# A transformer block with attention and feed forward: the output projection starts between the last values, and the feed forward's first half chunks stand under the last tile's normalisation

## What is computed

```python
mod = silu(c) @ wmod                        # sa, ca, ga, sb, cb, gb; |ga|, |gb| at least 0.25
h = layernorm(x) * (1 + ca) + sa
q, k, v = latent projections of h           # q from 128, k and v from 32 latent channels, rotary part of 64
attn = softmax(causal(q @ k.T * scale)) @ v # 32 heads
x = x + ga * (attn @ wo.T)                  # output projection
h = layernorm(x) * (1 + cb) + sb
gate = silu((h @ gate_w.T) * gate_s)        # 1376 hidden channels, int32 weights of -127..127
up = (h @ up_w.T) * up_s
x = x + gb * ((gate * up) @ down_w.T) * down_s
```

## Time and profile before

| | |
|---|---|
| time, median of 3 runs | 812.67 us (810.3 to 815.13) |
| profiled execution, its own time | 812.95 us |
| its span, first to last instruction | 810.8 us |
| granted TensorE clock over the span | 0.987 |
| TensorE busy | 759.1 us, 94% |
| VectorE busy | 553.5 us, 68% |
| ScalarE busy | 275.2 us, 34% |
| GpSimd busy | 152.5 us, 19% |

### The profile page before, as it was taken

The page is one execution under the profiler, slowest core; times in us unless marked ns, Lnnn a source line. Parts: engine busy times, 40 slices in busy tenths (PEclk is TensorE's granted clock), DMA queues, the critical chain, the costliest instruction groups (busy, mean ns, idle before and its releaser), DMA issues.

```text
span 810.8 us, 10303 instructions
## 1 busy us (share of the span) xinstructions
PE 759.1 (94%) x3901; PEld 497.4 (61%) x3901; DVE 553.5 (68%) x831; ACT 275.2 (34%) x394; POOL 152.5 (19%) x132
## 2 busy tenths in 40 slices
PE   3898899999999999999999999997997999999997
PEld 1755465555555555555555556453886788886886
DVE  6877679789789789789789779599464222223342
ACT  3722233433433433433433333444243222222210
POOL 1136413023023023023023000101242000000111
PEclk9999899999999999999999999999998999999999
DMA  8333613303303303303303380252000132210011
GB/s 307 155 78 78 149 23 78 86 9 79 85 9 79 86 9 78 80 15 79 84 10 79 71 342 3 105 209 78 1 1 0 50 107 78 78 30 0 27 40 39
DMA packets 36144, 60.72 MB, mean 75 GB/s; under 512 B 4256, under 2 KB 16288, under 8 KB 34304
## 3 DMA queue, kind: packets, MB, share of 16 engines
q1 hardware_dynamic: 36096, 60.06, 26.5%
HBM read 32.66 MB, written 2.10 MB: 43 GB/s over the span
## 4 chain that ended last, share of the span: by engine, by line
PE 53%; DVE 31%; issue 11%; POOL 3%; ACT 2%; DMA 1%; POOLq 0%; SPq 0%; DVEq 0%; ACTq 0%
PE PS L769 15%; DVE PR L1269 8%; DVE NMa L1172 7%; PE PS L739 6%; PE PS L612 5%; PE PS L675 5%; PE PS L690 4%; PE PS L676 4%; PE PS L677 4%; DVE NMb L1172 3%; DVE wide L1269 3%; PE PS L628 2%; PE PS L602 1%; PE PS L679 1%; PE PS L616 1%
## 5 line engine op out<-in xcount | busy, mean ns | idle before, releaser
L905 ACT ACTIVATE PR<-PS 128x1024 f32<-128x1024 f32 (+1 forms) x144 | 133.0, 929 | 258.1 <-PE PS L677 232.2
L1172 DVE TENSOR_REDUCE NMa<-PS 128x1 f32<-128x512 f32 (+3 forms) x216 | 137.8, 660 | 34.4 <-PE PS L616 31.0
L612 PE MATMUL PS<-KH,Q 96*128 96x512 f32 (+3 forms) x384 | 130.6, 400 | 3.5 <-DVE TQ L1157 1.5
L675 PE MATMUL PS<-Q,KH 97*128 97x512 f32 x288 | 130.7, 454 | 0.0
L769 PE MATMUL PS<-Q 128*128 128x512 f32 (+1 forms) x528 | 123.2, 395 | 5.1 <-DVE Q L1368 4.5
L769 PEld LDWEIGHTS PS<-Q 128*128 128x128 f32 (+1 forms) x528 | 99.3, 188 | 28.2 <-DVE Q L1368 4.7
L1269 DVE TENSOR_TENSOR PR<-PR 128x2048 f32<-128x2048 f32 (+3 forms) x56 | 110.4, 1971 | 6.9 <-ACT PR L905 5.5
L676 PE MATMUL PS<-Q,KL 96*128 96x512 f32 x288 | 114.3, 397 | 0.0
L677 PE MATMUL PS<-Q,KH 96*128 96x512 f32 x288 | 113.7, 395 | 0.0
L612 PEld LDWEIGHTS PS<-KH,Q 96*128 96x128 f32 x384 | 67.7, 191 | 56.0 <-issue 29.2
L675 PEld LDWEIGHTS PS<-Q,KH 97*128 97x128 f32 x288 | 55.9, 194 | 25.6 <-issue 13.7
(11 more groups left out here) (177 smaller groups left out, 944.4 us busy)
## 6 DMA issues: line engine op xcount, KB each, us to landing
Q<-TQ SPq DMA_DIRECT2D x64, 384.0 KB, 5.6
RT<-in_wo SPq DMA_DIRECT2D x4, 1024.0 KB, 4.9
TQ<-in_wo SPq DMA_DIRECT2D x4, 1024.0 KB, 4.8
WI<-in_gate_w SPq DMA_DIRECT2D x10, 256.0 KB, 3.3
WI<-in_up_w SPq DMA_DIRECT2D x10, 256.0 KB, 3.7
DI<-in_down_w SPq DMA_DIRECT2D x10, 256.0 KB, 3.8
PR<-in_wmod_c SPq DMA_DIRECT2D x2, 1024.0 KB, 6.5
x_in<-in_x SPq DMA_DIRECT2D x8, 256.0 KB, 9.7
```

The lines of the kernel that those rows point to most:

```text
L612: ins = pe.matmul(bank[:, i * w:(i + 1) * w], M.Q[0:KR, g % 2, 0, qt // 4, h0 + i, qs], M.KH[0:KR, lo:lo + w], start=(i == 0), stop=(i == ...
L675: pe.matmul(dst, M.KH[0:KR + 1, ks], M.Q[0:KR + 1, w % 2, 0, qb, :, qs], start=True, stop=False)
L905: act.activation(tiles, banks, ACT.Exp).then_inc(S_.p, 1)
L1172: dve.tensor_reduce(dst, PS[:, bank_of(turn), 0:n * w].rearrange("p (h k) -> p h k", k=w), axis=AX.X, op=ALU.max, negate=True).then_inc(S_ ...
```

## The change

- In the last window the planner's table gets `high` of tiles 0 and 1 at places 0.84 and 0.90, with cost 0: ScalarE makes the high part there, GpSimd (no longer VectorE) the low part. AH and AL move to other memory for this (`rotated`, over buffers of the rotary part, the folding and the floor).
- `products` is cut into thirds (`product_term`, 8 matmuls each) in banks of the side rotation. TensorE's order is: first third of product 0, values of step 10, second third, values of step 11, last third, denominators, then product 1 and on as before. `turn_hidden` uses banks 1 and 3.
- Chunk 0 of the feed forward is split between tiles 4 and 5 of the projection (its split weights lie where the keys were). Behind the turning of tile 6, TensorE makes the first half of the positions of chunk 0 (24 matmuls), the turning of tile 7, the first half of chunk 1, then both second halves. The split of chunk 1 stands ahead of tile 7's normalisation.
- Gate and up loads, and down loads, have semaphores of their own; SP waits for each apart.
- `down` uses banks 4 and 5; before it TensorE waits for chunk 9 only, and for the last chunk's down weights within tile 0.
- The last tile is scaled, added and stored in two halves of 256 columns; the second half is added on VectorE.

```diff
@@ -255,9 +258,11 @@
-        self.at = big
+        self.at = rotated
         self.AH = take("AH", [P, 2, G, P], F32R)
         self.AL = take("AL", [P, 2, G, P], F32R)
+        assert self.at <= folded_end
+        self.at = big
@@ -344,6 +351,7 @@
     if w == G - 1:
+        places += group_places(w, [(0.84 + 0.06 * st, ("high", st), 0.0) for st in range(2)])
@@ -508,18 +524,26 @@
-    load_chunk(0)
-    load_chunk(1)
+    for ch in range(2):
+        load_gates(ch)
+        load_down(ch)
     for ch in range(2, NCH):
         sp.wait_ge(S_.fl, ch - 1)
+        load_gates(ch)
         sp.wait_ge(S_.fdl, ch - 1)
-        load_chunk(ch)
...
+    sp.wait_ge(S_.ot, NS)
+    sp.dma_start(out[last, 0:D // 2], M.OT[:, 1, 0:D // 2]).then_inc(S_.st[1], 16)
+    sp.wait_ge(S_.oh, 1)
+    sp.dma_start(out[last, D // 2:D], M.OT[:, 1, D // 2:D]).then_inc(S_.st[1], 16)
@@ -724,20 +748,20 @@
-    for s in LATE_VALUES:
-        values(G - 1, s)
-    denominator(G - 1, 1)
...
+    def product_term(st, n):
+        b = st % 2
+        if n == 0:
+            pe.wait_ge(S_.al, st + 1)
+            if st >= 2:
+                pe.wait_ge(S_.yr, st - 1)
+        a, w = ((M.AH, M.MH), (M.AL, M.MH), (M.AH, M.ML))[n]
+        for g in range(G):
+            ins = pe.matmul(PS[:, out_bank(st), :], a[:, b, g, :], w[:, g, :], start=(n == 0 and g == 0),
+                            stop=(n == 2 and g == G - 1))
+        if n == 2:
+            ins.then_inc(S_.y, 1)
...
     for b in range(3):
-        pe.wait_ge(S_.free[b], (len(TURN) + 2 - b) // 3)
-    for st in range(NS):
-        products(st)
-        if st > 0:
-            turn_hidden(st - 1)
+        pe.wait_ge(S_.free[b], (len(TURN) + 1 - b) // 3)
+    for n, s in enumerate(LATE_VALUES):
+        product_term(0, n)
+        values(G - 1, s)
+    for n in range(len(LATE_VALUES), 3):
+        product_term(0, n)
+    denominator(G - 1, 1)
+    pe.wait_ge(S_.p, NEXP * G)
+    for st in range(1, NS):
+        for n in range(3):
+            product_term(st, n)
+        turn_hidden(st - 1)
...
             pe.wait_ge(S_.hl, 2 * st + 1 + rest)
+            if rest and st == 0:
+                pe.wait_ge(S_.fdl, NCH)
...
+    pe.wait_ge(S_.fl, 1)
+    pe.wait_ge(S_.lo2, NS // 2)
+    gate_up(0, 0)
+    turn_hidden(NS - 1)
+    pe.wait_ge(S_.fl, 2)
...
+    gate_up(1, 0)
+    pe.wait_ge(S_.lo2, NS)
+    gate_up(0, 1)
+    gate_up(1, 1)
...
+    pe.wait_ge(S_.fhid, NC)
+    pe.wait_ge(S_.fdl, NC)
@@ -961,31 +1014,32 @@
-    attn_high(0)
-    for st in range(NS):
-        if st < NS - 1:
+    for st in range(NS - 1):
+        if 2 <= st + 1:
             attn_high(st + 1)
         if st > 0:
             modulate2(st - 1)
-        if st < NS - 1:
-            root2(st)
+        root2(st)
+        if st == NS // 2:
+            chunk_high(0)
...
     act.wait_ge(S_.y, NS)
-    chunk_high(0)
+    chunk_high(1)
+    modulate2(NS - 2)
     root2(NS - 1)
-    chunk_high(1)
     modulate2(NS - 1)
@@ -1349,24 +1403,30 @@
     sums_copied(G - 1, 1)
     invert(G - 1, 1)
-    attn_low(0)
-    for st in range(NS):
-        if st < NS - 1:
+    dve.wait_ge(S_.al, 2)
+    for st in range(NS - 1):
+        if 2 <= st + 1:
             attn_low(st + 1)
         gated(st)
         if st > 0:
             h2_high(st - 1)
-        if st < NS - 1:
-            normalise2(st)
...
+        normalise2(st)
+        if st == NS // 2:
+            chunk_low(0)
+    gated(NS - 1)
+    chunk_low(1)
+    h2_high(NS - 2)
+    normalise2(NS - 1)
+    h2_high(NS - 1)
@@ -1420,6 +1477,9 @@
         gated2(st)
+    dve.wait_ge(S_.yr2, NS + 1)
+    dve.wait_ge(S_.st[1], 16 * (NS // 2 - 1))
+    dve.tensor_tensor(M.OT[:, 1, D // 2:D], M.x1[:, NS - 1, D // 2:D], M.Y2[:, 1, D // 2:D], ALU.add).then_inc(S_.oh, 1)
@@ -1513,6 +1573,14 @@
+    def attn_low_first(st):
+        pool.wait_ge(S_.gt, 8)
+        pool.wait_ge(S_.ah, st + 1)
+        pool.tensor_tensor(M.AL[:, st % 2], M.attn[:, :, st * P:(st + 1) * P], M.AH[:, st % 2].bitcast(F32),
+                           ALU.subtract).then_inc(S_.al, 1)
```

More of the change, by code:

```diff
@@ L726, in pe_program @@
                 side(name)
-    for s in LATE_VALUES:
-        values(G - 1, s)
-    denominator(G - 1, 1)
-    def products(st):
+    def product_term(st, n):
         b = st % 2
[L734 to L740, removed]
+        if n == 0:
[8 more added lines that the diff above has]
+            ins.then_inc(S_.y, 1)
     def turn_hidden(st):
@@ L747, in turn_hidden, with gate_up, gate_or_up @@
         for d in range(KD):
[L748 removed]
+            ins = pe.transpose(PS[:, 1 + 2 * b, d * P:(d + 1) * P], M.xn2[:, b, d * P:(d + 1) * P], M.ident[:])
         ins.then_inc(S_.tr2, 1)
     for b in range(3):
[L752 to L775 removed]
+        pe.wait_ge(S_.free[b], (len(TURN) + 1 - b) // 3)
[10 more added lines that the diff above has]
+        turn_hidden(st - 1)
+    def gate_up(ch, hf):
+        b, m = ch % 2, P if ch < NC else IT
+        for w in range(2):
+            gate_or_up(ch, hf, w, b, m)
+    def gate_or_up(ch, hf, w, b, m):
+        for n, (a, h) in enumerate(((M.FH, M.h2H), (M.FL, M.h2H), (M.FH, M.h2L))):
+            for k in range(KD):
+                ins = pe.matmul(PS[0:m, 4 * b + 2 * w + hf, :], a[b][:, w, k, 0:m],
+                                h[:, k, hf * 512:(hf + 1) * 512],
+                                start=(n == 0 and k == 0), stop=(n == 2 and k == KD - 1))
+        if hf == 1:
+            ins.then_inc((S_.fg, S_.fu)[w], 1)
     def down(st):
@@ L785, in down @@
                 for ch in chunks:
-                    ins = pe.matmul(PS[:, b, :], a[b][0:k, ch, :], w[0:k, ch, :],
+                    ins = pe.matmul(PS[:, 4 + b, :], a[b][0:k, ch, :], w[0:k, ch, :],
                                     start=(n == 0 and ch == 0), stop=(n == 2 and rest == 1))
         ins.then_inc(S_.y2, 1)
-    for ch in range(NCH):
-        gate_up(ch)
-    pe.wait_ge(S_.fhid, NCH)
-    pe.wait_ge(S_.fdl, NCH)
+    pe.wait_ge(S_.fl, 1)
[3 more added lines that the diff above has]
+    pe.wait_ge(S_.fl, 2)
+    pe.wait_ge(S_.yr, NS)
+    pe.wait_ge(S_.o, 2 * G)
+    for b in range(3):
+        pe.wait_ge(S_.free[b], (len(TURN) + 2 - b) // 3)
+    gate_up(1, 0)
+    pe.wait_ge(S_.lo2, NS)
+    gate_up(0, 1)
+    gate_up(1, 1)
+    for ch in range(2, NCH):
+        pe.wait_ge(S_.fl, ch + 1)
+        pe.wait_ge(S_.fhid, ch - 1)
+        b, m = ch % 2, P if ch < NC else IT
+        for w in range(2):
+            for hf in range(2):
+                gate_or_up(ch, hf, w, b, m)
+    pe.wait_ge(S_.fhid, NC)
+    pe.wait_ge(S_.fdl, NC)
     for st in range(NS):
@@ L886, in side, with attn_high @@
             split_high(key[1], key[2])
+        elif key[0] == "high":
+            attn_high(key[2])
+    def attn_high(st):
+        act.wait_ge(S_.no, 2 * (G - 1) + st * P // QB + 1)
+        if st == 0:
+            act.wait_ge(S_.side, TURN[("fold", G - 1, G - 1)] + 1)
+        if st >= 2:
+            act.wait_ge(S_.y, st - 1)
+        act.activation(M.AH[:, st % 2], M.attn[:, :, st * P:(st + 1) * P], ACT.Copy).then_inc(S_.ah, 1)
     def exponentials(w, e):
@@ L1350, in h2_high, with chunk_low @@
         dve.tensor_copy(M.h2H[:, :, st * P:(st + 1) * P], M.full2[:, st % 2]).then_inc(S_.hi2, 1)
+    def chunk_low(ch):
+        b, m = ch % 2, P if ch < NC else IT
+        dve.wait_ge(S_.fh, ch + 1)
+        dve.tensor_tensor(M.FL[b][:, :, :, 0:m], M.WI[:, b, :, :, 0:m], M.FH[b][:, :, :, 0:m].bitcast(F32),
+                          ALU.subtract).then_inc(S_.fl, 1)
     sums_copied(G - 1, 1)
     invert(G - 1, 1)
-    attn_low(0)
-    for st in range(NS):
-        if st < NS - 1:
+    dve.wait_ge(S_.al, 2)
+    for st in range(NS - 1):
+        if 2 <= st + 1:
             attn_low(st + 1)
@@ L1400, in gated2 @@
             dve.wait_ge(S_.ot, st - 1)
-        dve.scalar_tensor_tensor(out=M.Y2[:, b], in0=PS[:, b, :], scalar=M.ffn_s[:, 2:3], in1=M.gate_b[:],
-                                 op0=ALU.mult, op1=ALU.mult).then_inc(S_.yr2, 1)
-    chunk_low(0)
-    normalise2(NS - 1)
-    chunk_low(1)
-    h2_high(NS - 1)
+        for cols in (slice(0, D),) if st < NS - 1 else (slice(0, D // 2), slice(D // 2, D)):
+            dve.scalar_tensor_tensor(out=M.Y2[:, b, cols], in0=PS[:, 4 + b, cols], scalar=M.ffn_s[:, 2:3],
+                                     in1=M.gate_b[:, cols], op0=ALU.mult, op1=ALU.mult).then_inc(S_.yr2, 1)
     hidden(0)
@@ L1515, in side @@
             normalise(g, key[2])
+        elif kind == "high":
+            attn_low_first(key[2])
+    def attn_low_first(st):
[3 more added lines that the diff above has]
+                           ALU.subtract).then_inc(S_.al, 1)
     for st in range(NS + 1):
```

62 lines of the change are left out of this document (29 added, 33 removed).

## The result

The changed kernel takes **802.13 us** (median of 4 runs, 801.23 to 803.38), the kernel before beside it 813.65 (4 runs, 810.3 to 815.13): a ratio of 0.9866, 95% interval 0.9844 to 0.9888. It is faster. The forecast was 802.4. The execution that was profiled took 803.38 us around a span of 801.6, against 812.95 around 810.8: 9.2 us less of span, where the working of the prediction had 10.5.

A forecast was written before the change was run, and what follows sets the result against it. From 566.5 us the chain was taken as TensorE nearly throughout, with waits and slow-clock stretches to remove. Gains 1.5 - 0.7 + 7.8 + 1.4 + 0.5 = 10.5 took 812.95 to 802.4 us; range 797.5 to 805.8.

The forecast's parts named there:

- the feed forward's start: From product 7's end to the last gate matmul: 121.1 us instead of 128.94, 7.8 gained.
- down: Before the down matmuls: the first 30 no longer wait for the last chunk, 1.4 us gained.
- the last store: At the kernel's end: storing the last tile in halves puts the last issue 0.5 us earlier, 0.5 gained.
- The exclusion in the last window: End of attention: GpSimd's low parts and VectorE's two-SBUF-input work exclude each other, making the last additions 3.6 us late.
- Rival 2: End of attention: GpSimd's low parts cost VectorE nothing, product 2 starts 2.3 us earlier, 797.9 us; chance 0.10.
- the one from product 1 to product 2: Projection's start: gating to normalisation takes 4.2 us, and product 2 starts at 576.8 instead of 580.29.
- Chunk 0's split: Mid-projection, after tile 4's root: the earlier split delays the low part of tile 6, 0.7 us lost once.
- The clock: Around products 0 and 1: one fall to half clock in the new gaps, at the old price, 2.3 us lost.
- rival 1: Gaps around products 0 and 1: no fall of the clock, 2.3 us better, 800.2 us; chance 0.33.
- rival 3: Gaps around products 0 and 1: two clock falls, 3.2 and 2.3 us, giving 805.7 us; chance 0.12.
- Rival 4: End of attention: a late GpSimd low part blocks the values behind product 0's first third, 804.4 to 806.4 us; chance 0.04.
- Rival 5: Projection: the clock falls at 561 and is not regained, matmuls take twice as long, up to 841 us; chance 0.02.

The follow-up runs named there:

- run 7: Changed kernel with TensorE's old order behind product 7 (tile 7 turned after 12 matmuls, whole chunks), chunk 0's early split kept: 806.93 us.
- run 6: Changed kernel with the old end: TensorE waits for the last chunk before down, and the last tile is scaled, added and stored whole: 805.49 us.
- run 12: The changed kernel measured again, unedited: 803.19 us, ratio 0.9879 to the kernel before.
- run 1: Changed kernel with the low parts of tiles 0 and 1 on VectorE instead of GpSimd, at the same places: 802.11 us.
- run 3: Changed kernel with GpSimd's two low parts cut from 128 to 8 columns per head group, products 0 and 1 reading the high part instead: 799.98 us.
- run 2: Changed kernel with a one-column dummy square root behind ScalarE's last copy, to load the function table early: 804.9 us.
- run 4: Changed kernel with products 1 to 5 in PSUM banks 0 and 2: 801.64 us.
- run 8: Changed kernel with AH and AL starting at a multiple of 512 bytes in their new place: 802.61 us.
- run 9: Changed kernel with the splits of tiles 2 to 7 back at their old SBUF place, tiles 0 and 1 at the new one: 803.6 us.
- run 5: Changed kernel with chunk 0's early split in two halves, after tile 3 and after tile 4: 801.56 us.
- run 10: Changed kernel with low parts of tiles 0 and 1 on VectorE, early table load and chunk 0's split in halves: 798.21 us, ratio 0.9812 to the kernel before.
- run 11: The version of run 10 with the splits of tiles 2 to 7 also at their old SBUF place: 799.1 us, ratio 0.9822 to the kernel before.

## Why the prediction was right, and where not

**The direction and the size** came from the terms for the feed forward's start, for down and for the last store, which all held. The feed forward's start was to gain 7.8 and gained 8.1; run 7 splits it in two nearly equal halves. The stretch is 120.83 us, 121.1 forecast. The cover was close, as said: tile 7's normalised rows stood 5.5 us after product 7 (forecast 5.6, needed by 5.9). The wait before down gave 1.42 (1.4), and 0.3 more in down itself, since TensorE no longer restarts there (run 6). The halves of the store gave 0.61 (0.5); run 6 alone 0.64.

**The exclusion in the last window** was costed by the earlier trace rows and held: from the values of step 9 to the start of product 1 10.64 us at full clock was forecast (558.16 to 568.8), and run 12, with no fall there, has 10.64 (558.21 to 568.85). That they agree to the hundredth is luck: the pause is 1.7 and not 2.3, and the matmuls around it take 0.6 more than forecast. Rival 2 is out, and its price is known: runs 1 and 3 have 18.35 to product 2 against 20.12, so 1.8, not 2.3.

**The step that failed is the one from product 1 to product 2.** It had "gating to normalisation 4.2 (574.45 to 578.62, rows 5)", and with it product 2 at 576.8, 8.0 behind the denominators. Run 12 has 9.5. The 4.2 came from a tile for which the table load was already done. In the kernel before, ScalarE's two copies stood ahead of the first root and the load ran behind them, under other work (564.33); the change moves both copies into the last window, and now the load stands behind ScalarE's wait for the moments (why it is put there, and was put ahead of it before, the runs do not show). The code does not name the load. The trace of before did, in a timeline of ScalarE that I read only up to the exponentials. VectorE's wait for the root is 1.72 us instead of 0.36: 1.4 of the 1.5 missing. Run 2 gets 1.03 of it back, and the rest, 0.36 of waiting with the load long done, no run explains. About 0.1 is in the small steps of the chain ahead of it.

**Not foreseen either: the slower products.** The step "takes 5.47, not 5.76" took product 2's time at its old pace. The 5.76 stood behind a short wait too: tile 2's low part ended at 580.22 and the product's first matmul started at 580.27, and the change does not take that wait away. With 5.60 for each of products 2 to 7 and 0.26 more for each restart behind a wait (5.86 for products 2 and 6), this stretch lost 1.45 where 0.4 was forecast. Runs 4 and 8 exclude the bank and the alignment to 512 bytes, run 9 shows the place. Chunk 0's split cost 0.5 of waiting at product 6 (0.7 forecast) plus that restart.

**The clock.** One fall was forecast at 2.3 us; it was one, at 1.5 (21.62 against 20.12, or 7.39 against 5.86). In no profiled execution of a version with both pauses (after and runs 2, 4, 5, 6, 7, 8, 9 and 12) was there none, as rival 1 had it, and in none were there two at these pauses (rival 3): six had it behind the first pause, three behind the second (run 7's other fall, at 622, belongs to its own pause). Of the four versions without the first pause, three had none (runs 1, 10, 11) and one had it at the second (run 3). So the first pause costs 1.8 by itself, and a fall of 1.5 came in all nine executions that have it, against one of four without it; one execution of each version is few to put a chance on that. The Trainium skill (TensorE: Matmul & The Clock Gate, What's actually happening) says that the point at which the clock changes varies with how the work lies to a window that runs freely; after and run 12, one program with the fall at 564 and at 578 us, fit this. Rivals 4 and 5 did not come: the low part was there in time, and the clock was back after 3 to 4 us. (Rival 5's 841 does not follow from its words: 46 us of matmuls taken twice as long on top of 800.2 are 846.)

**How the number came out right.** Against the profiled execution the working is 1.0 us too good (802.4 for 803.4). The step errors are larger than that: 1.4 for the table load and what stays of its wait, 0.1 for the chain, 1.1 for products and restarts, 0.3 for the later last window, and on the other side 0.8 for the clock, 0.3 for the feed forward, 0.3 for down and 0.1 for the store; the execution also has 0.4 less around its span than the one before. Part of the closeness is luck of signs. The kernel was measured at 802.13 and again at 803.19.

**Theories.** A holds: runs 1, 2 and 5 gave 3.3 (with the fall), 1.0 and 0.5, a sum of 4.8, and together, in run 10, 4.76 (58.43 to 53.67) on the way to the end of product 7. B holds only at product 6 of run 9. The version of run 10 beats the changed kernel: 0.9812 with an interval of 0.9798 to 0.9825 against 0.9866 and 0.9879, whose intervals begin at 0.9844 and 0.9862, about 4 to 5 us.

## What to carry to other kernels

When instructions of ScalarE are moved away from ahead of a function change, look up the table load in its timeline and ask what it will stand behind; a dummy call of the next function in a gap took 1.0 of its 1.4 us off the path here. Moving 1.2 us of work off VectorE to an idle GpSimd can cost more than it saves where VectorE works on two SBUF tensors at the same time: here two low parts were 2.44 us on VectorE and 3.4 us of delay on GpSimd. Compare stretches between fixed points of the program rather than spans, where the clock's falls shift whole traces by more than the effect.

## What the hardware showed that was not expected

- A place in SBUF sets the pace of matmuls: 24 matmuls with a 128x128 stationary operand took 5.60 us at the new place and 5.47 to 5.50 at the old one, same shapes (run 9 against after; within run 9, 1.87 us for 8 matmuls of product 1 at the new place, 1.83 for product 2 at the old one). Neither the bank nor an alignment to 512 bytes changed it. Which property of the place does it was not found.
- A wait of TensorE cost 0.26 to 0.29 us more than its idle time: 5.86 for 5.60 behind idle times of 0.51 and 0.77 at full clock, 60.33 for 60.04 in down.
- A fall of the clock moves between two pauses 15 us apart in executions of one program, at the same price of 1.5 us at either, so that totals alone do not show where it stood.
